# Local attention on one core: the order of TensorE's pieces around the value projections, and which PSUM bank each projection uses

## The reference

```python
def attn_layer(x, Wqkv, qs, ksc, Wo):
    q, k, v = split(x @ Wqkv)              # 128 -> 3 x 1024
    q = l2norm(q) * qs;  k = l2norm(k) * ksc
    q = q * cos * scale + rotate_half(q) * sin * scale
    k = k * cos * inv   + rotate_half(k) * sin * inv
    out = local_attention(q, k, v)         # window 32, softmax
    return out @ Wo
```

## Time and profile before

| | us |
|---|---|
| time, median of 3 runs (lowest, highest) | 4612.93 (4612.48, 4614.09) |
| span of the profiled execution | 4612.9 |
| TensorE busy | 4249.6 |
| vector engine busy | 3755.0 |
| scalar engine busy | 3499.8 |
| GpSimd busy | 3200.2 |

### The profile page before, as it was taken

How to read it: one execution, slowest core, us unless ns; L and a number is a source line. 1 busy time by engine, 2 the same in 40 slices (tenths; PEclk the granted TensorE clock), 3 DMA queues, 4 the chain that set the end, 5 groups by cost and what they waited for, 6 DMA issues and landing times. The chain is left out here.

```text
span 4612.9 us, 154012 instructions
## 1 busy us (share of the span) xinstructions
PE 4249.6 (92%) x51351; PEld 2797.3 (61%) x51353; DVE 3755.0 (81%) x9044; ACT 3499.8 (76%) x12855; POOL 3200.2 (69%) x4297
## 2 busy tenths in 40 slices
PE   6949999999999999999999999999999999777885
PEld 3426656665666656666566665666656666455543
DVE  4779899994999849997599966999669995688497
ACT  6948788883888838898488875888658886588434
POOL 2522299993999839997499975999659995344162
PEclk8969999999999999999999999999999999788986
DMA  2000000000000000000000000000000000000000
GB/s 62 0 21 1 6 2 0 0 1 25 2 0 0 1 25 2 0 0 19 7 2 0 0 20 6 2 0 0 20 7 1 0 0 20 1 0 0 28 0 19
DMA packets 36135, 34.48 MB, mean 7 GB/s; under 512 B 11302, under 2 KB 31012, under 8 KB 34852
## 3 DMA queue, kind: packets, MB, share of 16 engines
q1 hardware_dynamic: 35876, 31.13, 2.2%
HBM read 29.03 MB, written 2.10 MB: 7 GB/s over the span
## 5 line engine op out<-in xcount | busy, mean ns | idle before, releaser
L2238 ACT ACTIVATE local_prob<-ps,local_shift_by 128x128 f32<-128x128 f32 x3072 | 1078.5, 377 | 3.3 <-DVE local_shift_by L2330 3.2
L2166 POOL TENSOR_TENSOR local_qk<-local_qk,local_rsin 128x512 f32<-128x512 f32 x768 | 968.0, 1271 | 43.4 <-DVE local_rsin L2355 43.4
L2173 POOL TENSOR_TENSOR local_qk<-local_qk,local_inv 128x512 f32<-128x512 f32 x768 | 792.3, 1043 | 131.2 <-ACT local_inv L2257 130.5
L2497 PE MATMUL ps<-local_wqkv,local_xsT 128*128 128x512 f32 x1536 | 798.4, 604 | 10.6 <-DVE local_rsin L2355 5.2
L2180 POOL TENSOR_TENSOR local_prob<-local_prob,local_rs 128x512 f32<-128x512 f32 x768 | 789.9, 1040 | 12.2 <-DVE local_rs L2337 12.2
L2238 ACT ACTIVATION_READ_ACCUMULATOR local_prob<-ps,local_shift_by 128x1 f32 x3072 | 671.9, 219 | 0.0
L2330 DVE TENSOR_REDUCE local_shift_by<-ps 128x4 f32<-128x512 f32 x768 | 524.8, 683 | 81.3 <-PE ps L2575 80.8
L2355 DVE TENSOR_TENSOR local_rsin<-ps,local_sin_t 128x256 f32<-128x256 f32 x1536 | 572.0, 414 | 0.0
L2344 DVE TENSOR_TENSOR local_qk<-ps,local_cos_t 128x512 f32<-128x512 f32 x768 | 525.2, 684 | 35.8 <-ACT local_sq L2246 34.4
L2246 ACT ACTIVATE local_sq<-ps 128x512 f32<-128x512 f32 x768 | 466.7, 608 | 76.7 <-PE ps L2497 38.9
L2362 DVE TENSOR_REDUCE local_ss<-local_sq 128x8 f32<-128x512 f32 x768 | 513.3, 670 | 4.0 <-ACT local_sq L2246 4.0
(11 more groups left out here) (338 smaller groups left out, 8768.6 us busy)
## 6 DMA issues: line engine op xcount, KB each, us to landing
local_wqkv<-L_ffn_Wqkv SPq DMA_DIRECT2D x7, 1536.0 KB, 6.2
local_wo<-L_ffn_Wo SPq DMA_DIRECT2D x7, 512.0 KB, 7.0
out<-quantised_res SPq DMA_DIRECT2D x8, 256.0 KB, 2.3
local_w<-L_ffn_W SPq DMA_DIRECT2D x6, 341.0 KB
early_L_decay<-c_decay SPq DMA_DIRECT2D x1, 1024.0 KB, 10.7
local_w<-L_ffn_W SPq DMA_DIRECT2D x12, 64.0 KB
load_raw<-L_ffn_w SPq DMA_DIRECT2D x8, 64.0 KB, 2.0
local_b<-L_ffn_b SPq DMA_DIRECT2D x24, 0.5 KB
```

Of the source, the lines that this page charges most:

```text
L2166: nc.gpsimd.tensor_tensor(qk[w][:, j, :, :], qk[w][:, j, :, :], rsin[j % 2][:, :, :], ALU.add).then_inc(rot_ready, 1)
L2173: nc.gpsimd.tensor_tensor(qk[w][:, j, :, :], qk[w][:, j, :, :], bcast(inv[:, w, 8 * j:8 * j + 8].unsqueeze(2), [P, 8, LH]), ALU.mult).then ...
L2238: last = nc.scalar.activation(prob[w][:, g, j, :], ps[:, 4 + g % 2, j * P:(j + 1) * P], ACT.Exp, bias=shift_by[:, w, h:h + 1], accum_out=s ...
L2497: nc.tensor.matmul(proj_bank(j), xsT[w][:, :], wqkv[:, 512 * j:512 * j + 512], start=True, stop=True).then_inc(proj_ready, 1)
```

## The change

The banks of the q/k projections go from (1, 0, 0, 1) to (0, 1, 0, 1). On TensorE one step becomes: transposes of q/k 0, projection 2 (of the block whose projections 0 and 1 were in the step before), output, projection 3, transpose of x, probability transposes 1, weighted values 0, scores 0, transposes of q/k 1, weighted values 1, value projections 0 and 1, projection 0, shift, projection 1, probability transposes 0, scores 1. The waits follow the new order. On the scalar engine the copy of value half 1 moves ahead of `squares(·, 0)`, and `squares(·, 2)` moves from before `exponentials(·, 2)` to behind it. The lists of the vector engine and of GpSimd stay as they are.

```diff
-    UNIT_BANK = (1, 0, 0, 1)
+    UNIT_BANK = (0, 1, 0, 1)
...
                 exponentials(n + 3, v, 0, live)
+                evacuate_values(n + 3, v, 1, live)
                 squares(n + 5, v, 0, live)
...
                 evacuate_probs(n + 2, u, 0, 0, live)
-                evacuate_values(n + 3, v, 1, live)
                 log_variance(n - 1, v, live)
+                evacuate_qk(n + 4, u, 0, 0, live)
+                over_deviation(n - 1, v, live)
+                exponentials(n + 3, v, 2, live)
                 squares(n + 5, v, 2, live)
-                over_deviation(n - 1, v, live)
-                evacuate_qk(n + 4, u, 0, 0, live)
-                exponentials(n + 3, v, 2, live)
                 exponentials(n + 3, v, 3, live)
...
                     if j == 0:
                         pe.wait_ge(xsT_ready, b + 1)
-                        wait(pe, rot_step, 4 * b)
...
                         wait(pe, vals_ready[0], b - 1)
...
-                    elif j == 2:
-                        wait(pe, rot_step, 4 * b + 2)
...
-                    else:
+                    elif j == 1:
                         wait(pe, vals_ready[1], b - 1)
...
+                    elif j == 2:
+                        wait(pe, rot_step, 4 * b + 1)
+                    else:
+                        wait(pe, rot_step, 4 * b + 2)
...
                     pe.wait_ge(xvT_ready, b + 1)
...
+                    wait(pe, rot_step, upto(4 * b + 7 + half, 4 * NB))
...
                 turn_qk(n - 2, u, 0, live)
+                project(n - 1, v, 2, live)
                 output(n - 5, v, live)
                 project(n - 1, v, 3, live)
...
                 turn_qk(n - 2, u, 1, live)
+                weighted_values(n - 4, u, 1, live)
                 project_values(n - 2, u, 0, live)
+                project_values(n - 2, u, 1, live)
                 project(n, u, 0, live)
                 shift(n - 5, v, live)
                 project(n, u, 1, live)
-                weighted_values(n - 4, u, 1, live)
                 turn_probs(n - 3, v, 0, live)
-                project_values(n - 2, u, 1, live)
-                project(n, u, 2, live)
                 scores(n - 2, u, 1, live)
```

More of the change, by code:

```diff
@@ L2485, in project @@
                             wait(pe, rot_step, 4 * b - 1)
-                            wait(pe, rot_step, 4 * b - 2)
-                    elif j == 2:
-                        wait(pe, rot_step, 4 * b + 2)
-                        if isinstance(b, int):
-                            wait(pe, vals_ready[0], b - 1)
-                            wait(pe, rot_step, 4 * b - 1)
-                    else:
+                    elif j == 1:
                         wait(pe, vals_ready[1], b - 1)
                         if isinstance(b, int):
-                            wait(pe, rot_step, 4 * b + 1)
                             wait(pe, rot_step, 4 * b)
+                    elif j == 2:
+                        wait(pe, rot_step, 4 * b + 1)
+                    else:
+                        wait(pe, rot_step, 4 * b + 2)
                     nc.tensor.matmul(proj_bank(j), xsT[w][:, :], wqkv[:, 512 * j:512 * j + 512],
@@ L2502, in project_values @@
                     pe.wait_ge(xvT_ready, b + 1)
[L2503 to L2512, removed]
+                    wait(pe, rot_step, upto(4 * b + 7 + half, 4 * NB))
+                    if isinstance(b, int):
+                        wait(pe, vals_ready[half], b)
                     nc.tensor.matmul(ps[:, half, :], xvT[w][:, :],
```

## The result

The changed kernel takes 5080.77 us (median of 5 runs, 5076.43 to 5085.88) against 4612.93 (a median of 5 runs too, not of 3 as the table ahead has it): a ratio of 1.1014, 95% interval 1.1001 to 1.1028. The forecast was 4862, range 4800 to 4910. The direction was right, the size was missed: +468 us where +249 were forecast. The profiled execution has a span of 5078.5 us, 465.6 more than the earlier trace rows.

The account below looks back on a forecast made before the run. TensorE was taken to bound the kernel; its loop step would grow from 14.46 to 16.0 us. 1.54 x 27 steps = 41.6 a layer, x 6 = 249 us, so 4613 + 249 = 4862 us, range 4800 to 4910.

Parts of the forecast that it names:

- What bounds the kernel before: Block loop: TensorE sets the pace at 14.46 us a step, with 1.48 us of slack before scores 1.
- Scores 1 close behind projection 1: TensorE: scores 1 start 3.25 us after projection 1, waiting for exponentials 1; TensorE stands for 1.60 us.
- Projection 0 behind the value copy: TensorE: projection 0 waits for the vector engine's copy of value half 0, 0.20 us in a step.
- The saving of one run of full-array work: TensorE: grouped value projections and output product take 3.61 us instead of 3.80, a gain of 0.19 in a step.
- The vector engine, second chain: Vector engine: two waits grow, before cosines 0 and the sum of squares 2; it needs at most 15.9 us a step.
- the step of 16.0: TensorE's loop step after the change: 3.25 + 12.52 + 0.20 = 15.97, taken as 16.0 us, 1.54 longer than 14.46.
- Edits that cost nothing: Scalar-engine copy of value half 1 moved earlier, bank order, shortened waits: no cost; squares 2 priced on the vector engine.
- Start and end of a layer: Outside the 27 full steps: zero, between -2 and +3 us a layer at the start; zero at the end.
- Rival D: Short TensorE pauses in the loop could let the clock swing; chance 0.06, no time given.
- B: Vector engine sets the pace, smaller wait on the exponentials: 15.3 to 15.6 a step, 4749 to 4798 us; chance 0.06.
- C: Scores do not wait and one full-array run less counts: 4576 to 4615 us; chance 0.05.
- A: The forecast itself: TensorE waits at scores 1 in each step, 4812 to 4910 us; chance 0.83.

Follow-up runs that it names:

- experiment 9: Kernel before the change with two extra scalar-engine copies ahead of exponentials 1: 4624.10 us, ratio 1.0026.
- experiment 2: Changed kernel with exponentials 1 ahead of squares 1 on the scalar engine: 5249.96 us.
- experiment 3: Changed kernel with projection 2 put back on TensorE ahead of scores 1, scalar engine's list as changed: 5029.56 us.
- experiment 1: Changed kernel with squares 2 back ahead of exponentials 2 on the scalar engine: 5017.11 us.
- experiment 12: Changed kernel with the nine filler matmuls of step 2 moved in front of the wait at each layer's start: 5054.77 us.
- kernel 7: Kernel before the change with weighted values 1 moved from behind projection 1 to in front of the value projections: 4801.54 us, ratio 1.0409.
- kernel 5: Changed kernel with projection 2 back ahead of scores 1 and squares 2 ahead of exponentials 2: 4906.54 us.
- 8: Kernel before the change with projection 2 moved beside the output product and squares 2 behind exponentials 2: 4650.58 us, ratio 1.0082.
- kernel 10: Changed kernel with projection 2 back ahead of scores 1, squares 2 first, heads copied early, plus two scalar-engine copies ahead of exponentials 1: 5000.50 us.
- experiment 4: Changed kernel with the transpose of x moved on TensorE from behind projection 3 to behind weighted values 0: 5029.71 us.

## Why the prediction was wrong

*What bounds the kernel before*: right. TensorE sets the step, with slack before scores 1: experiment 9 put 0.96 of the 1.48 to use without a cost. Of the 1.48 the hand-over to the scores is a part (0.15 in the changed kernel, from 1585.62 to 1585.77), so some 1.3 can be spent, an estimate.

*Scores 1 close behind projection 1*: right (3.25). That it fits to the hundredth is luck: the exponentials were done 3.10 after projection 1 where 3.06 was forecast, and the hand-over took 0.15 instead of 0.19. And this wait does not set the step: experiment 2 made it shorter and the kernel slower, experiment 3 moved 0.86 us of work into it and the step stayed. *Projection 0 behind the value copy*: forecast 2.03 after value projection 0, measured 1581.41 - 1579.41 = 2.00. *The saving of one run of full-array work* is there: output takes 1590.24 - 1588.45 = 1.79, as forecast. It is paid back at projection 0.

*The vector engine, second chain*: its two waits had the right sizes (0.80 before the sum of squares 2; 1.11 before cosines 0, forecast 1.0), but the step that failed is the conclusion drawn from them. The forecast treated the vector engine as a loop of its own, needing at most 15.9, and TensorE as another, needing 16.0, and took the larger. The two are joined: the transpose of x waits for the residual. The loop that sets the step runs from projection 0 over the scalar engine into the vector engine's list, from its end back to TensorE, and round to projection 0. Counted from projection 0 (1581.41): cosines 0 start after 1.85, maxima 2 4.63 later, the sum of squares 2 2.75 later (forecast 2.7), the residual 0.60 after that, the transpose of x 0.42 after it. That is 10.25, or 9.14 after projection 1, where TensorE alone would be at 8.6. With 7.62 behind it the step is 16.76. The forecast had the two longer waits; the length of the list between them stands in the trace of the kernel before, but it never followed them into the transpose.

Of the 0.77 that the step of 16.0 is short, 0.57 is this wait. Another 0.13 is the piece after the pause before the scores: from line 2554 to the next transposes of q/k it is 1.08 (1585.77 to 1586.85), where the step of the earlier trace rows took 0.95 (from 1505.11). Projection 0 itself takes 0.94 to the shift instead of 0.86 (1581.41 to 1582.35).

*Edits that cost nothing*: wrong for squares 2, which the forecast priced on the vector engine only, where it found them to fit. Squares 2 behind exponentials 2 cost 0.57 a step in the changed kernel (experiment 1).

*Start and end of a layer: zero*: the second step that failed, +5.3 and +9.7 us a layer (2.3 of the latter is the last block's own step). The start is mostly the filler (experiment 12 returns 3.4 of the 5.3), and it goes with the granted clock. Over the first five steps of the second layer, in the kernel before, the changed one and that of experiment 1:
```profile
1129.70:1191.30 61.60, 54.20 (x526) 28.89 (x526) 51.75 (x119) 39.90 (x147) 47.07 (x49) 0.97 0.05 11
...
1203.60:1270.60 67.00, 55.51 (x526) 30.43 (x526) 51.75 (x118) 40.73 (x150) 47.51 (x51) 0.92 0.04 10
...
1192.60:1263.80 71.20, 58.91 (x526) 32.16 (x526) 51.88 (x118) 39.89 (x145) 47.56 (x51) 0.88 0.04 9
```
The same five steps take 64.0 at 0.95 in experiment 12. In the tail the pieces moved away from before the scores leave the same hole, 2.05 us there:
```profile
1735.52 0.43 PE L2554 MATMUL ps<-band,identb 64*64 64x256 bf16 x4 [2.05 <-ACT local_prob L2238]
1735.63 1.60 PE L2560 MATMUL ps<-local_qkT 64*64 64x64 f32 x32
```

*Rival D, the clock*: in part true, far below its price. The long steps, 12 of 138, are the ones in which the granted clock fell: 0.57 over 1452 to 1456, some 1.1 us lost each (17.9 against 16.77), 3 us a layer with those from block 5 on. The forecast's sentence that no row of the loop showed such a fall held for the kernel before only. The Trainium skill, page "TensorE: Matmul & The Clock Gate", section "A second HAM failure mode: psum-queue depth-cycling", says of another kernel that frequent short idle times between groups of matmuls made the clock swing; these 12 steps agree with that, the other 126 do not show it.

*Rivals B and C*: neither time came. B had the engine half right (the vector engine's list is on the path that sets the step) but expected a shorter step, not a longer one. The upper end of A's range should read 4915, not 4910 (4613 + 284 + 18); it changes nothing.

The sum in terms of the forecast: 249 for the loop by 1.54 a step. Measured: 2.31 in 26 steps is 360, the clock 18, starts 32, tails 58, together 468. So of the 219 us missed, 111 lie in the loop, most of them in the joint of the two engines, and 108 in terms that the forecast had put at zero; either alone would have left the range.

What each part of the change costs, by a ladder of kernels from the one before to the changed one: weighted values 1 early 0.9 a step (kernel 7); the value projections side by side, with their banks, waits and scalar-engine copy, 0.6 on top (kernel 5, which besides places squares 2 a little differently; these edits were not taken apart); squares 2 behind exponentials 2 0.9 (kernel 3); projection 2 beside the output product 0.0 (the changed kernel). The order of such a ladder matters: on the kernel before, the last two cost 0.2 together (8).

## What to carry to other kernels

In a schedule written out by hand a piece is also the cover of every wait behind it. Before moving one away, list the waits of all that then moves up (here the exponentials, two banks, the residual), not only the nearest. And follow the path that crosses engines until it returns to its first piece: two engines whose loops each look just short enough (15.9 and 16.0 here) can be tied by one wait, and the loop that runs through both (16.77) then decides. The longest pause on the busiest engine need not be on that loop: here the pause of 1.53 before the scores was not, and the short one of 0.40 before the transpose of x was. A filler belongs in front of the wait it covers, and has to be looked at again when the order changes.

## What the runs showed that was not expected

TensorE's granted clock stayed at its upper level in all 138 loop steps of kernel 3, where TensorE is busy 323.6 of 360 us (1320 to 1680) with its idle time split into waits of 0.42 to 0.65, and in all of kernel 10, with a pause of 0.95 besides one of 0.43. In the changed kernel, busy 318.1 of 360 us with a pause of 1.53 and one of 0.40 in each step, it fell in 12 of the 138 steps; with the pause of 1.53 also in experiment 1 (7 steps), experiment 4 (18) and experiment 12 (14). It is not the pause of 1.53 alone: in experiment 2, whose longest is 0.99 and which has three more of 0.54 to 0.74, it fell in 8. The pauses are alike in every step of a kernel; why it falls in these steps and not in the others is left open.
